# Neighbour sums of a graph layer: items of one 128-edge tile against items of two, in both chunks

## The reference

```python
xn = _layernorm(x)
agg = jax.ops.segment_sum(xn[dst], src, num_segments=6250)   # edge_index = [src, dst]
cnt = jax.ops.segment_sum(ones, src, num_segments=6250)
gnn = xn @ W1.T + b1 + (agg / max(cnt, 1)) @ W2.T + b2
x = x + gnn + mix(xn)                # mix: per-head layernorm, k^T v, q (k^T v)
x = x + ffn(_layernorm(x))           # 8 experts, top 1, capacity 977
```

## Time and profile before

| what | value |
|---|---|
| median of 3 runs | 1998.8 us (1995.85 to 1999.64) |
| the profiled execution | 1998.75 us, its span 1997.1 us |
| sort of chunk 0, table of x | 0 to 305 us |
| gathers of chunk 0 (392), sort of chunk 1 beside them | 305 to 836.6 us |
| gathers of chunk 1 (438), heads and own products | 836.6 to 1414 us |
| nodes, router and experts | 1417 to 1997 us |
| busy: PE, DVE, ACT, POOL | 1529.7, 1367.3, 710.2, 985.5 us |

### The profile page before, as it was taken

The page is one execution under the profiler, slowest core; times in us unless marked ns, Lnnn a source line. Parts: engine busy times, 40 slices in busy tenths (PEclk is TensorE's granted clock), DMA queues, the critical chain, the costliest instruction groups (busy, mean ns, idle before and its releaser), DMA issues. The chain is left out here.

```text
span 1997.1 us, 27369 instructions
## 1 busy us (share of the span) xinstructions
PE 1529.7 (77%) x6558; PEld 885.3 (44%) x6558; DVE 1367.3 (68%) x3735; ACT 710.2 (36%) x1954; POOL 985.5 (49%) x969
## 2 busy tenths in 40 slices
PE   4599995667778777365665558798593999999997
PEld 2255542233333333133333335454482766666665
DVE  8998997889998988476666657666781433444344
ACT  4488890008787876000000002111281222222221
POOL 0000006777777777777777777777263111111111
PEclk7699997679999998555555558878655999999999
DMA  6980013333333333743333334444464123323200
GB/s 185 180 151 32 32 36 86 98 100 94 99 98 97 95 96 98 86 123 100 101 100 101 98 111 131 127 132 127 140 226 163 41 96 97 105 96 103 101 9 5
DMA packets 101500, 204.49 MB, mean 102 GB/s; under 512 B 19794, under 2 KB 64760, under 8 KB 99392
## 3 DMA queue, kind: packets, MB, share of 16 engines
q0 software_dynamic: 49488, 131.52, 23.6%
q1 hardware_dynamic: 43164, 64.16, 12.1%
q10 hardware_dynamic: 8700, 7.07, 1.2%
HBM read 157.43 MB, written 49.89 MB: 104 GB/s over the span
## 5 line engine op out<-in xcount | busy, mean ns | idle before, releaser
L511 POOL DMA_INDIRECT w<-xn_parts,idx x830 | 856.4, 1032 | 260.8 <-issue 236.4
L1018 DVE TENSOR_TENSOR XA<-XA,bank 128x257 f32 x878 | 367.3, 418 | 280.9 <-PE bank L765 250.1
L764 PE MATMUL bank<-w,S 128*128 (+1 forms) x878 | 294.0, 337 | 275.0 <-SPq L461 114.6
L764 PEld LDWEIGHTS bank<-w,S 128*128 128x128 f16 x878 | 93.4, 106 | 486.8 <-issue 301.1
L765 PE MATMUL bank<-w,S 128*128 (+1 forms) x878 | 298.2, 342 | 0.0
L1800 POOL DMA_INDIRECT out<-ob,tok x64 | 66.5, 1040 | 401.2 <-DVE ob L1786 384.9
L596 ACT ACTIVATE LV<-LH,v 125x128 f16<-125x128 f16 x600 | 182.5, 388 | 195.8 <-DVE LH L1268 195.5
L1724 PE MATMUL bank<-w,ht 128*117 128x256 f32 (+1 forms) x1024 | 223.7, 379 | 0.0
L1713 PE MATMUL bank<-xt,w 128*128 128x468 f32 (+1 forms) x512 | 214.8, 578 | 0.8 <-ACT xt L1738 0.8
L1748 ACT ACTIVATE ht<-bank,b1c 128x468 f32<-128x468 f32 (+1 forms) x128 | 85.6, 669 | 333.4 <-PE bank L1713 333.4
L1724 PEld LDWEIGHTS bank<-w,ht 128*117 128x117 f32 (+1 forms) x1024 | 188.8, 186 | 30.5 <-issue 0.4
(11 more groups left out here) (290 smaller groups left out, 2326.0 us busy)
## 6 DMA issues: line engine op xcount, KB each, us to landing
w<-f SPq DMA_DIRECT2D x16, 1024.0 KB, 7.6
w<-xn_parts,idx POOLq DMA_INDIRECT x830, 2.8
expert_rows<-XA SPq DMA_DIRECT2D x2, 6296.5 KB, 62.7
xb<-expert_rows SPq DMA_DIRECT2D x8, 1028.0 KB, 11.4
xb<-expert_rows SPq DMA_DIRECT2D x8, 939.7 KB
XA<-x SPq DMA_DIRECT2D x6, 1024.0 KB, 5.6
xn_parts<-w POOLq DMA_DIRECT2D x12, 512.0 KB, 3.3
work<-x ACTq DMA_DIRECT2D x48, 128.0 KB, 2.2
```

The source lines that it names most:

```text
L511: pool.indirect_dma_start(ring[:, o:o + 2 * D], None, tab, bass.IndirectOffsetOnAxis(ap=idx[:, t:t + 1], axis=0)).then_inc(s_g[t % RING], 16)
L764: pe.matmul(psA[t % AR][:, 0:AGW], lhs, ring_high[:, ds(o, AGW)], start=True, stop=True)
L1018: v.tensor_tensor(XA[:, ds(o, AGW)], XA[:, ds(o, AGW)], psA[t % AR][:, 0:AGW], ALU.add).then_inc(s_ev, 1)
```

## The change

Chunk 0 becomes dense too, by the same code as chunk 1: 44,000 edges in 344 tiles. An item is now two neighbouring tiles (a "two") and a block: 172 twos and 220 items in chunk 0, 219 twos and 267 items in chunk 1. An item takes four products (high and low part of both tiles) into one bank, and one addition. In a border item the columns of S that belong to other blocks are zero. `source_onehots` still makes 8 one-hots at a time, which are now those of 4 items. The instruction counts that follow: gathers 830 to 782, additions 878 to 487, products 1756 to 1948, one-hots 110 to 122. SyncE counts twos, and does so in chunk 0 too. The steps of the program are halves of items: 440 beside chunk 1's sort (392 tiles before), 534 in chunk 1 (486 before). The tile one-hots of chunk 0's sort, and the products with them, have 344 columns instead of 392.

```diff
-    for cols, padded in ((352, True), (448, False)):
-        tiles = (cols * EP + NB * (P - 1)) // P if padded else -(-cols * EP // P)
+    for cols in (352, 448):
+        tiles = -(-cols * EP // P)
...
-T0 = CHUNKS[0][3]
-DENSE = -(-COLS1 * EP // P)
-ITEMS = DENSE + NB - 1
-IW = -(-ITEMS // SB) * SB
-AHEAD = 16
+DENSE = tuple(-(-c[1] * EP // (2 * P)) * 2 for c in CHUNKS)
+TWOS = tuple(n // 2 for n in DENSE)
+ITEMS = tuple(n + NB - 1 for n in TWOS)
+SI = SB // 2
+T0, G0 = ITEMS[0], DENSE[0]
+STEPS0, STEPS1 = 2 * ITEMS[0], 2 * ITEMS[1]
+AHEAD = 8
@@ side_plan
-    for t in range(T0):
+    for t in range(STEPS0):
-        while k < len(costs) and spent < total * (t + 1) // (T0 - RING):
+        while k < len(costs) and spent < total * (t + 1) // (STEPS0 - GR - SB):
@@ SyncE
-        for t in range(T0, T0 + DENSE):
-            sp.wait_ge(s_g[t % RING], 16 * (t // RING + 1))
-            sp.sem_inc(s_land, 1)
...
+        def landed(two):
+            for u in (2 * two, 2 * two + 1):
+                sp.wait_ge(s_g[u % RING], 16 * (u // RING + 1))
+            sp.sem_inc(s_land, 1)
+        def let_go(two):
...
+            sp.wait_ge(s_tile, last[i % GR] & 1023)
+            sp.sem_inc(s_free, 1)
+        for two in range(sum(TWOS)):
...
+            landed(two)
+            if AHEAD <= two < sum(TWOS) - RING // 2 + AHEAD:
+                let_go(two - AHEAD)
@@ GpSimd
-        for t in range(T0 + DENSE):
-            if t in (0, T0):
-                pool.wait_ge(s_dec, 1 if t == 0 else 2)
-            if t >= RING and t % 2 == 0:
-                if t < T0 + RING:
-                    pool.wait_ge(s_tile, t + 2 - RING)
-                else:
-                    pool.wait_ge(s_free, t - T0 + 2 - RING)
+        for u in range(sum(DENSE)):
+            if u in (0, G0):
+                pool.wait_ge(s_dec, 1 if u == 0 else 2)
+            if u >= RING and u % 2 == 0:
+                pool.wait_ge(s_free, (u + 2 - RING) // 2)
@@ TensorE, sum_tile(q), half h = q % 2 of item t = q // 2
+            if h == 0:
+                if i == 0:
+                    pe.wait_ge(s_rows, c + 1)
+                if i % GR == 0:
+                    item[:] = [...]        # 2 x 16 values into registers
+                pe.wait_ge(s_land, item[1][i % GR] & 1023)
...
+            pe.matmul(psA[t % AR][:, 0:AGW], lhs, ring_high[h][:, ds(o, AGW)], start=(h == 0), stop=True, ...)
+            ins = pe.matmul(psA[t % AR][:, 0:D], lhs, ring_low[h][:, ds(o, D)], start=False, stop=True, ...)
+            if h == 1:
+                ins.then_inc(s_tile, 1)
@@ VectorE
-        def place(pp, pq):
...
-        def place_dense():
+        def place_dense(c, pp, pq):          # chunk 0 by it too
...
-        def decode(c):
...
-            step(v.tensor_tensor(idx[:, ch0:ch0 + tiles], d, e, ALU.bitwise_or))
-            step(v.tensor_scalar(a, b, 255, None, ALU.bitwise_and))
-            v.tensor_copy(srcl[:, ch0:ch0 + tiles], a).then_inc(s_dec, 1)
+        def decode_dense(c, gap):            # chunk 0 by it too, with gap 0
+            v.memset(halves[:, :, tiles // 2:2 * P], 0.0)
+            v.tensor_copy(ident16, ident[:, :])
...
+            v.tensor_tensor(idx[:, u0:u0 + tiles], d, e, ALU.bitwise_or).then_inc(s_dec, 1)
...
-        for t in range(T0):
-            tile(t)
-            while ran < SIDE[t]:
+        for q in range(STEPS0):
+            if q % 2 == 0:
+                item_sum(q // 2)
+            while ran < SIDE[q]:
```

More of the change, by code:

```diff
@@ L751, in sum_tile @@
                 if i % GR == 0:
[L752 removed]
+                    many = min(GR, ITEMS[c] - i)
                     item[:] = [nc.values_load_multi_w_load_instructions(
                         row[:, i:i + many], engines=[mybir.EngineType.PE], min_val=low, max_val=high,
[L755 to L756 removed]
@@ L1117, in place_dense @@
+            step(v.scalar_tensor_tensor(out=used16[0:1, :] if c else two_used[0], in0=pp[0:1, 0:twos], scalar=float(t0),
+                                        in1=iota_t[0:1, 0:twos], op0=ALU.add, op1=ALU.add))
             wait()
@@ L1277, in second_chunk @@
                 yield
[L1278 removed]
+            yield from decode_dense(1, GAP)
             yield
```

352 lines of the change are left out of this document (161 added, 191 removed).

## The result

The changed kernel takes 1960.9 us (median of 4 runs, 1960.1 to 1963.8) against 1998.1 us of the kernel before (1995.9 to 1999.6): a ratio of 0.9816, 95% interval 0.9803 to 0.9829, or 37 us less. I had forecast 1945, with 1928 to 1961 as the range; the sign is right, the saving forecast is too large by 16 us, and the time lies at the very end of the range. The profiled execution took 1960.8 us with a span of 1959.2.

A forecast was written before the change was run, and what follows sets the result against it. GpSimd's gathers were taken as the bound, their count times 1.34 us each. Summed: -60.0 + 6 + 4.1 - 4 + 0 + 0.5 = -53.4 us on 1998.75, giving 1945, with 1928 to 1961 as the range.

The forecast's parts named there:

- 12 x 0.5 = +6: VectorE's one-hots of the sums: 12 more, each lengthening gathers by 0.5 us, +6 us, between 0 and 14.6.
- the plain price: Each of the 48 removed gathers gives back 0.946 + 0.30 = 1.25 us, -60.0 us; with lengthening counted in, -64.3.
- the mean price goes with each gather: Rival: gathers get cheaper too, each removed one giving back 1.34 us; about 1928 us, chance 0.12.
- the likeliest case: The forecast of 1945 us itself, chance 0.70, with its terms' own bounds said to add up to 1930 to 1962.
- the additions "as nothing": VectorE's additions fall from 878 to 487, 164 us of its time, counted as nothing because VectorE is not waited for.
- Chunk border: Between the chunks, GpSimd's slack before chunk 1's `idx` is needed falls from 39 to 21 us, costing nothing.
- The rival of the late sort: Chunk 1's sort comes late and GpSimd stands at the border; an 8% loss costs 15 us, 1960; chance 0.13.
- Place step: VectorE's place step of chunk 0, ahead of everything, grows from 4.5 to 8.6 us: +4.1, between +3 and +6.
- sort of chunk 0: Chunk 0's sort, ahead of the first gather, has 344 columns for 392: -4 us, bounds -11 and 0.
- Register loads: TensorE's new register loads in chunk 0, 14 loads making 30 us, are hidden and cost nothing.
- Tail: After the last gather, an item of two tiles needs two more products: +0.5 us.
- Chunk 0's chain as the bound: Rival: the item chain paces chunk 0's gathers; break-even 3.06 us a two, at 3.2 the kernel takes 2022; chance 0.05.

The follow-up runs named there:

- run 1: The changed kernel with the sums' one-hots made tile by tile, with one SBUF input each; 1926.6 us, ratio 0.9641.
- run 2: The kernel before with the sums' one-hots made tile by tile, with one SBUF input each; 1955.4 us, ratio 0.9784.
- run 3: As run 1, with the lane one-hots of chunk 1's sort also made with one SBUF input; 1923.2 us, ratio 0.9630.
- 5: The changed kernel with one-hots made for four halves instead of eight, 244 in place of 122; 1927.1 us, ratio 0.9642.
- 9: The kernel before with one-hots of four tiles instead of eight; 1972.7 us, ratio 0.9866.
- run 6: The changed kernel with one-hots made behind the wait for the item's products, just ahead of the addition; 1963.0 us, ratio 0.9826.
- Run 8: The changed kernel with one more VectorE instruction, a never-read copy within PSUM, for each of chunk 0's 220 items; 1998.3 us, ratio 0.9997.
- run 4: The changed kernel's dense places in both chunks, but items of one tile again, with 878 additions; 1993.2 us, ratio 0.9973 against the kernel before.
- 10: The changed kernel with one-hots of four and chunk 1's lane one-hots made with one SBUF input; 1927.7 us, ratio 0.9646.
- 12: As run 3, with the chunks cut at 368 and 432 columns instead of 352 and 448; 1908.5 us, ratio 0.9559.
- run 7: The changed kernel with chunk 0's register loads written twice, though the second loads are not in the program that ran; 1965.1 us, ratio 0.9829.

## Why the prediction was right and wrong

**Right: what bounds, and what a gather gives back.** The count of gathers times their price was the number to read. The median and the gap of 0.30 us did not move, there is no hole on GpSimd, and 48 x 1.25 = 60 us came back. Between 307 and 1378 us GpSimd waits for nobody but in 12 waits of 3.7 us in all.

**Wrong: the one-hots, "12 x 0.5 = +6".** This is the term that failed, and with it the choice "I take the plain price, since the one-hots do not go with the gathers", which froze the price of all others. Measured is +23.2 us. By the split above the one-hots of the sums rose from 47.6 to 65.9 us, from 0.43 to 0.54 us each: 12 new ones at the old price are 5 us, nearly as forecast, and the new price of all 122 is the other 13. The lane one-hots, for which the sum had no term, rose by 8.0 us, all in chunk 0; the other two-input instructions and the rest fell by 3. That such compares carry it is shown by runs 1 to 3, that their price falls faster than their length by 5 and 9, and that the moment moves it by run 6 (15 us in the profiles, where one program's two profiles differ by 5). That the new beat of an item of two tiles is what spoiled it is inferred, from chunk 1's prices: 0.34 and 0.42 us with items of one tile, 0.48 to 0.60 with items of two. The bound "0 to 14.6" for the 12 new ones held for those, and the sum had no bound for the old ones. The forecast's own rival, that the mean price goes with each gather, had the sign of this wrong. The bounds of the likeliest case were also added up wrongly: as listed they give 1945.3 - 18.1 = 1927 to 1945.3 + 19.5 = 1965, not 1930 to 1962.

The rule of the Trainium skill, SBUF — State Buffer, section Who interferes with whom, that a VectorE instruction with two SBUF inputs contends with a GpSimd one that reads SBUF, agrees with runs 1 to 3. The same section calls the shared ports an exclusive lock, and the trace agrees with that too: a gather that starts under such an instruction waits until 0.13 us before its end. It was my reading that went too far, 1.22 us for each one-hot: a one-hot costs only when a gather starts under it, and then what is left, 0.43 to 0.54 us of 1.217 averaged over all one-hots. The forecast also cited the section as if one SBUF input always left GpSimd alone. It counts `tensor_scalar` among the operations that can take both ports; run 3 shows gathers lengthened beside rows of such compares, while the 976 of run 1 with 275 ns each cost 0.8 us.

**Half wrong in its reason: the additions "as nothing".** The number came out, since GpSimd has no hole and TensorE and VectorE only follow. But the text took that as a property of the kernel before and after. Run 8 shows that it is not one: 73 us more of VectorE in chunk 0's stretch of the changed kernel lengthen it by 37 us. I had compared VectorE's 452 of 530 us with 100%. The share is a poor measure in either direction, since run 2 did the same work in 469 us and run 4 took 517. Without the halved additions the 48 gathers brought 5 us in run 4, which has 22 more register loads in chunk 0 as well; which of the two took the rest isn't shown.

**Chunk border.** Forecast 21 us in hand, measured 10, "still nothing". It is right for this kernel and was near its end: runs 1, 3, 4, 6, 8, 10 and 12 all lost 10 to 15 us there. The rival of the late sort had the right place and the wrong kernel.

**Place step** +4.5 for +4.1, **sort of chunk 0** -3 for -4 (the first gather came 1.7 us later), **relay of SyncE** 3.7 us in 12 waits as before: as forecast. **Register loads** hold no gather (3.7 us of slot waits in all); more of them were not tried. **Tail** -3.0 for +0.5: a wait of 4.69 us for TensorE's next block became 0.43 us; I had looked at the last item and not at what stands behind it. It hid 3.5 us of the miss, which is luck.

**Chunk 0's chain as the bound** (2022) did not come; at 485.3 / 172 = 2.82 us a two it stands 0.24 us below the point of 3.06 that I had named. Run 8, at 522.5 / 172 = 3.04 us, came to that point and measured 0.9997, in agreement with it.

Two things stay open. Nothing shows why chunk 1's row numbers come between 775 and 791 us in ten of the 14 kernels, whatever was taken from VectorE (the others: 797.3 before, 797.0 in run 6, 824.9 in run 4, 829.0 in run 8): which hand-over sets it I did not isolate. And the register loads of chunk 0, with the waits for landings that came with them, were never varied alone.

## What to carry to other kernels

Price the bound engine's instruction as it runs there, with what the others do to it: a change that takes instructions away from it and shifts the beat of its neighbours moves the price of all that remain, and that term (17 us here) can be a third of the gain forecast. An engine that nobody waits for can still stand close behind the bound; its busy share does not say how close (VectorE did about the same work in 469 us in one kernel and in 517 in another), but adding work to it does (run 8). After each gain look again at the hand-over with the smallest slack, because that is where the next one goes. Where an added instruction changes nothing, count it in the trace before calling it hidden (run 7).

## What the runs showed of the hardware

- A gather costs 0.946 us and 0.30 us of gap. If an instruction of VectorE with two SBUF inputs runs when it starts, it is lengthened by what is left of that instruction less 0.13 us: 1.74 us under a 1.21 us compare with 0.93 us left, 0.99 us with 0.17 us left, 1.20 us under a multiplication with 0.38 us left, and within 0.015 us in 339 of 346 cases in the two kernels. The instruction itself keeps its length: the one-hots' median is 1.215 to 1.218 us in every tenth of the gather's first 1.2 us in which they begin.
- With one SBUF input it is nearly the other way round. Run 3's 128x128 one-hots take 0.244 to 0.248 us (medians by tenths) when they begin in the first 0.4 us of a gather and 0.434 us (median of 74) when they begin 0.5 to 0.6 us after its start, while the gather is not held; but rows of such compares did hold gathers that started under them, by up to 0.7 us.
- Eight times as many instructions can be cheaper for the neighbour: 976 compares by a value a lane are 26 us more work for VectorE than 122 large ones, and 63 us less for GpSimd.
- The same compare in two halves (683 ns for 1217) costs 34 us less, with 18 us more work for VectorE.
- Loading 16 values into TensorE's registers takes 1.1 us; where two such loads stand ahead of a sum, TensorE is idle for up to 2.2 us (run 4).
